# A graph layer and a routed feed-forward layer on one core: message rows gathered before they are normalized, full expert tiles started from eight queues, results scattered out between the gathers

## The chip, the cores and the metric

The kernel runs on one core of one Trainium2 chip. The metric is the device time in microseconds (us) of one execution; the time of a kernel is the median of its runs.

## The reference

All values are 32-bit floats. There are 12,500 nodes with 256 features and 212,500 edges, sorted by destination.

```python
x = x + gnn(layernorm(x))
x = x + ffn(layernorm(x))

def gnn(features):                      # src, dst, edge_weight: 212500 each
    msgs = features[src] * edge_weight[:, None]
    agg = segment_sum(msgs, dst, 12500)
    return agg @ W.T + b

def ffn(h):                             # 8 experts, 256 -> 1024 -> 256
    idx = argmax(softmax(h @ gate_w + gate_b));  prb = that probability
    pos = place of the token among those of its expert, in order
    y = relu(h @ w1[idx] + b1[idx]) @ w2[idx] + b2[idx]
    return nan_to_num(y * prb * (pos < capacity))
```

## The kernel before

Nodes are handled in 98 tiles of 128. The edges are cut into 98 groups of 17 columns of 128 edges, and each group into three thirds of 6, 6 and 5 columns. The kernel has these parts:

- **Normalizing x (prologue).** SP loads batches of 7 tiles of x, DVE takes their moments (`moments`, L1076 and L1081), ACT scales them (`normalize`, L786) and stores them to the DRAM tensor `normed`. POOL clears the accumulator `aggT` (L688) meanwhile. POOL waits until all of `normed` is stored and for the flag of a check of the edge lists (L690, L691) before its first gather.
- **Aggregation.** For each column, POOL issues one indirect DMA (`gather`, L707) that fetches 128 rows of `normed` into `msg`. DVE copies the indices into `idx` (L1193) and builds the weighted one-hot matrices of a third with two operations (`prep`, L1195, L1199). PE multiplies (`sub`, L939), ACT copies the sums out (`pair_out`, L846), PE transposes them (L948) and DVE adds them to `aggT` (L1216).
- **Node.** For a finished tile PE multiplies by W (`gnn`, L957), DVE adds x and bias and normalizes (L1225 to L1241), PE transposes (L966) and computes the gate (L972), DVE chooses the expert (`route_a`) and works out the row (`route_b`, L1264 to L1276), and POOL scatters the tile's rows into the DRAM tensor `rows_by_expert` (`scatter`, L714). SP stores the sum x + gnn to the DRAM tensor `x_after_gnn` (L621).
- **Experts.** The 98 node tiles form four segments of 25, 25, 25 and 23. When a segment is routed, DVE plans it (`planning`), and its expert tiles (118 slots with padding in all) run beside the gathers of the next segment: rows loaded by SP into `hin` (L573), transposed on PE (L990), layer 1 (L999), relu on ACT (L810), layer 2 (L1011), bias on DVE (L1290), and stored by ACT to one of the DRAM tensors `expert_outputs` (L826). Weights are loaded by SP (L584) into one of two slots of `wsl` if the expert changes. `hin` has two buffers too; a row load waits for the transpose two tiles before (`s_ft`, L572).
- **Combining.** After the last segment is planned, six node tiles at a time: SP loads `x_after_gnn` (L629), POOL gathers the rows of `expert_outputs` (L735), DVE multiplies and adds (L1302), ACT checks for NaN (L834) and stores to the output (L837).

The order of work is written out in Python by `steps_of`, and every engine walks the same list (`walk`). Each engine executes its own instructions strictly in that order, and a wait on a semaphore holds up everything behind it on its engine. `s_route` tells POOL that a tile's rows have their places; `s_y` that an expert tile's result is in `yrow`.

Of the kernel before, what the change touches and what calls it, by code (L numbers as in the profile page):

```python
# [5 lines left out]
P = 128  # L13
# [6 lines left out]
WIN = 64  # L20
LAG = 2
# [3 lines left out]
EXTRA = 2  # L25
LN_TILES = 7
LN_BUFS = 4
MOST_FINS = 6

C_IDENT, C_TRI, C_IOTA, C_HALVES, C_ODD, C_RANK, C_SEG = 0, 128, 256, 320, 384, 448, 456  # L30


def segments_of(tiles):

    if tiles >= 90:
        last = [25, 25, 23]
        return [tiles - sum(last)] + last
    return [tiles - tiles // 2, tiles // 2]
# [6 lines left out]
def layout_of(n, e, experts):  # L45

    tiles = -(-n // P)
    edge_tiles = -(-e // P)
    group = -(-edge_tiles // tiles)
    third = -(-group // 3)  # L50
    subs = [third, third, group - 2 * third]
    halves = [[-(-n // 2), n // 2] for n in subs]
    seg = segments_of(tiles)
    caps = [P * (t + 1) for t in seg]
    base = [0]
    for c in caps:
        base.append(base[-1] + (experts + 1) * c)
    columns = -(-(n + WIN) // WIN) * WIN

    fins = min(MOST_FINS, columns // (4 * P))  # L60
    return dict(tiles=tiles, aggregate=columns, fins=fins, group=group, subs=subs, halves=halves, seg=seg, caps=caps, base=base,
                columns=(tiles + 1) * group, ffn=[t + experts - 1 for t in seg])


def buffer_of(s, last):

    return 2 if s == last else min(s, 1)


def paces_of(products, iterations):  # L70

    for pattern in ([2, 3, 3], [3, 3, 3], [4, 4, 3], [4, 4, 4]):
        paces = [2] + [pattern[j % 3] for j in range(iterations - 1)]
        if sum(paces) >= products:
            return paces
    return paces


def steps_of(tiles, seg, ffn, per_step):

    steps = [dict(agg=0), dict(agg=1)]  # L90
    node = f = k0 = place = 0
    last = len(seg) - 1
    ends = [seg[0], sum(seg[:last]), tiles]
    products, paces = [], [0] * tiles

    def plan_products(s):

        end = k0 + ffn[s] - EXTRA
        for k in range(k0, end):
            first = [("turn", k)] if k == k0 else []  # L100
            ahead = k + 2 < end
# [20 lines left out]
    for s, t in enumerate(seg):  # L122
        for j in range(t):
# [3 lines left out]
            if node:  # L127
                it["rank"] = node - 1
# [1419 lines left out]
```

## Time and profile before

| | us |
|---|---|
| median of 3 runs | 2694.51 (2691.34 to 2696.41) |
| the profiled execution, its own time | 2699.82 |
| its span, first to last instruction | 2697.8 |
| first gather starts | 127.98 |
| last gather starts | 2361.51 |
| POOL busy | 1822.4 (68% of the span) |
| PE busy | 1910.5 (71%) |
| mean granted TensorE clock | 0.822 |

A row of a table of groups reads: line, engine, operation, what is written <- what is read, shape, how often | busy us, mean ns of one | idle time of the engine just before them and what ended it. A row of a timeline reads: start, duration, engine, line, operation, how often, and in brackets the idle time before and its releaser. PEld is the load of weights into PE, SPq and ACTq are the issue of a DMA by SP and ACT. Busy shares are averages over stages with different limits, so the rows below are taken stage by stage.

### The profile page before, as it was taken

How to read it: one execution, taken by the hardware profiler on the slowest of the kernel's cores; microseconds unless marked ns; L12 is line 12 of the kernel's file. 1: busy time of each engine (PE TensorE's matmuls, PEld its weight loads, DVE VectorE, ACT ScalarE, POOL GpSimd, SP SyncE). 2: the span in 40 equal slices, each digit the busy share in tenths (PEclk: the TensorE clock that was granted, in tenths of full speed). 3: DMA queues.
4: the chain of work that ended last, by engine and by line, in shares of the span. 5: the costliest groups of instructions: out<-in, count | busy, mean ns of one | idle time of the engine just before them, and what ended most of it. 6: DMA issues, size and time to landing. Idle time of an engine off the chain costs nothing. (4 is left out here: it accounts for less than half of the span.)

```text
span 2697.8 us, 41267 instructions
## 1 busy us (share of the span) xinstructions
PE 1910.5 (71%) x11208; PEld 1430.3 (53%) x11208; DVE 1157.6 (43%) x4700; ACT 853.0 (32%) x2232; POOL 1822.4 (68%) x1867
## 2 busy tenths in 40 slices
PE   0045556666568888888678888887688888849992
PEld 0023333333346666666466666665467666638882
DVE  6524443443454444444444444444544444442222
ACT  2502221222223333333233333333233333314443
POOL 3077777777777777777777777777777777722333
PEclk9976665555569898988689889898798999969996
DMA  5733333333366464455465644654665446447775
GB/s 202 263 109 115 116 116 115 117 116 116 116 203 198 132 198 130 132 194 163 132 231 167 197 130 132 196 165 124 213 195 198 138 143 207 142 110 248 241 270 155
DMA packets 207538, 444.34 MB, mean 165 GB/s; under 512 B 48332, under 2 KB 133572, under 8 KB 197372
## 3 DMA queue, kind: packets, MB, share of 16 engines
q0 software_dynamic: 89376, 244.09, 30.7%
q1 hardware_dynamic: 84744, 156.38, 16.9%
q10 hardware_dynamic: 33172, 41.08, 4.2%
q8 instruction: 95, 1.56, 0.2%
q14 instruction: 151, 1.24, 0.1%
HBM read 374.71 MB, written 72.43 MB: 166 GB/s over the span
## 5 line engine op out<-in xcount | busy, mean ns | idle before, releaser
L707 POOL DMA_INDIRECT msg<-normed,idx x1666 | 1604.1, 963 | 613.4 <-issue 507.3
L939 PE MATMUL ps_agg<-msg,onehot 128*64 128x256 f32 x3332 | 611.2, 499 | 501.1 <-DMA msg<-normed,idx 458.6
L939 PEld LDWEIGHTS ps_agg<-msg,onehot 128*64 128x64 f32 x3332 | 288.0, 171 | 718.9 <-DMA msg<-normed,idx 540.4
L999 PE MATMUL ps_h<-hTf,wsl 128*128 128x128 f32 x3776 | 473.4, 286 | 3.9 <-DVE hTf L1283 3.9
L999 PEld LDWEIGHTS ps_h<-hTf,wsl 128*128 128x128 f32 x3776 | 459.4, 202 | 25.4 <-issue 18.7
L1011 PE MATMUL ps_y<-wsl,hmid 128*128 128x256 f32 x1888 | 444.6, 390 | 5.3 <-ACT hmid L810 5.3
L1011 PEld LDWEIGHTS ps_y<-wsl,hmid 128*128 128x128 f32 x1888 | 362.0, 197 | 54.9 <-issue 7.3
L1216 DVE TENSOR_TENSOR aggT<-aggT,ps_agg 128x128 f32 x588 | 169.6, 288 | 488.8 <-PE ps_agg L948 253.5
L810 ACT ACTIVATE hmid<-ps_h,wsl 128x128 f32<-128x128 f32 x944 | 268.3, 370 | 311.7 <-PE ps_h L999 305.9
L846 ACT COPY pairs<-ps_agg 128x256 f32<-128x256 f32 x294 | 107.9, 367 | 655.6 <-PE ps_agg L939 655.3
L1193 DVE COPY idx<-src_sb 128x6 int32<-128x6 int32 (+1 forms) x297 | 68.4, 230 | 422.4 <-PE ps_agg L939 415.7
L735 POOL DMA_INDIRECT aggT<-expert_outputs,yidx x98 | 98.6, 1006 | 178.6 <-DVE yidx L1295 110.5
L1290 DVE TENSOR_TENSOR yrow<-ps_y,wsl 128x256 f32<-128x256 f32 x118 | 50.0, 424 | 303.1 <-issue 149.5
L867 ACT ACT_TABLE_LOAD x97 | 124.5, 1283 | 136.7 <-DVE yrow L1290 135.4
L1199 DVE TENSOR_TENSOR onehot<-onehot,wgt 128x384 f32<-128x384 f32 (+1 forms) x297 | 160.0, 539 | 10.2
L948 PE MATMUL ps_agg<-cst,pairs 128*128 128x128 f32 x588 | 137.4, 321 | 30.2 <-ACT pairs L846 30.0
L1195 DVE TENSOR_TENSOR onehot<-cst,rel 128x384 f32<-128x384 f32 (+1 forms) x297 | 157.1, 529 | 0.0
L714 POOL DMA_INDIRECT rows_by_expert<-hrow,slot_i x98 | 98.3, 1003 | 67.5 <-DVE slot_i L1276 38.6
L857 ACT COPY aggS<-aggT 128x256 f32<-128x256 f32 x98 | 39.6, 404 | 280.1 <-DVE aggT L1216 280.1
L957 PE MATMUL ps_x<-wg_sb,aggS 128*128 128x256 f32 x392 | 126.6, 455 | 0.0
L860 ACT ACT_TABLE_LOAD x98 | 125.7, 1283 | 2.6 <-ACTq L887 0.9
L948 PEld LDWEIGHTS ps_agg<-cst,pairs 128*128 128x128 f32 x588 | 84.4, 169 | 76.1 <-ACT pairs L846 67.0
(130 smaller groups left out, 1501.8 us busy)
## 6 DMA issues: line engine op xcount, KB each, us to landing
wsl<-in_w SPq DMA_DIRECT2D x72, 1024.0 KB
msg<-normed,idx POOLq DMA_INDIRECT x1666
hin<-rows_by_expert SPq DMA_DIRECT2D x118, 128.0 KB
expert_outputs<-yrow ACTq DMA_DIRECT2D x118, 128.0 KB, 2.5
xt<-in_x SPq DMA_DIRECT2D x97, 128.0 KB
x_after_gnn<-xt SPq DMA_DIRECT2D x97, 128.0 KB
aggT<-x_after_gnn SPq DMA_DIRECT2D x97, 128.0 KB, 3.8
out_x<-aggT ACTq DMA_DIRECT2D x97, 128.0 KB, 2.9
```

Source lines behind the costliest of these rows:

```text
L707: pool.indirect_dma_start(out=msg[:, j, :], out_offset=None, in_=ln_dram, in_offset=bass.IndirectOffsetOnAxis(ap=idx[:, j:j + 1], axis=0)) ...
L810: ins = nc.scalar.activation(hmid[:, c, :], ps_h[:, c, :], ACT.Relu, bias=b1_at(b)[:, c:c + 1])
L860: nc.scalar.activation(rt[:, 2 * E8:3 * E8], rt[:, E8:2 * E8], ACT.Exp, accum_out=sc[:, 1:2]).then_inc(s_exp, 1)
L867: nc.scalar.activation(sd[:, :], mv[:, 1:2], ACT.Sqrt, bias=eps[:, 0:1]).then_inc(s_sd, 1)
L939: ins = nc.tensor.matmul(ps_agg[h * WIN:(h + 1) * WIN, q % 2, 0:D], onehot[:, j, :], msg[:, j, :], start=i == 0, stop=i == HALVES[q][h] - 1)
L948: last = nc.tensor.transpose(ps_agg[:, q % 2, D + k * P:D + (k + 1) * P], pairs[:, q % 2, k * P:(k + 1) * P], ident)
L957: last = nc.tensor.matmul(ps_x2[:, 0:D], aggS[:, k, :], wg_sb[:, k, :], start=k == 0, stop=k == KD - 1)
L999: last = nc.tensor.matmul(ps_h[:, c, :], w1_at(b)[:, q, c * P:(c + 1) * P], hTf[:, q, :], start=q == 0, stop=q == KD - 1)
L1011: last = nc.tensor.matmul(ps_y[:, 0:D], hmid[:, c, :], w2_at(b)[:, c, :], start=c == 0, stop=c == FC - 1)
L1195: dve.tensor_tensor(hot, iota.unsqueeze(1).to_broadcast([P, n, WIN]), rel[:, bass.ds(col, n)].unsqueeze(2).to_broadcast([P, n, WIN]), ALU. ...
L1199: dve.tensor_tensor(hot, hot, wgt[:, bass.ds(col, n)].unsqueeze(2).to_broadcast([P, n, WIN]), ALU.mult).then_inc(s_onehot[q], 1)
L1216: dve.tensor_tensor(columns, columns, half, ALU.add).then_inc(s_added[q] if h else s_half, 1)
```

## The change

The kernel's file is rewritten in large part; what it computes is the same.

- **Start.** POOL's first gathers wait only for the first 34 columns of the indices. The first 12 groups (36 thirds, 204 gathers) fetch rows of `x` itself; DVE takes the moments of each gathered row and ACT normalizes it in `msg` (`message_moments`, `normalize_messages`). Meanwhile x is normalized to `normed` in 25 batches of 4 tiles, interleaved with these thirds; from third 36 on the gathers fetch from `normed`. ACT and DVE clear `aggT`.
- **Aggregation.** `msg` is a ring of four thirds. Gathers take their index straight from `src_sb`. The one-hot matrix of a column is 32 wide and made by one `tensor_scalar` with two scalars per row (17 for a group), four quarters of a third are multiplied side by side, and the transpose becomes a product with a shift matrix (`turn`), so that one addition per third goes to `aggT`.
- **Nodes.** They start at third 38, one every two thirds until they have caught up (node 32, about third 104), then one every three thirds. Rows are 260 wide: x + gnn, its two normalizing factors, the gain and the node's number; POOL scatters them into eight queues in DRAM, one per expert. `x_after_gnn` goes.
- **Experts.** There are no segments. A visit v takes 128 rows of one queue: `plan` (11 small DVE operations) picks the fullest queue, or the one of two visits before while it still has 128 rows, whose weights are then kept. Visits start with node 13; each takes two thirds (layer 1, layer 2): one every two thirds up to third 104, then one for a node, and from node 68 on five for four nodes. There are 105 visits; in the list of events 85 of them (0 to 84) have their layer 2 inside the 294 thirds, and 20 (85 to 104) after the last third. Before visit 89, SP writes 8 pads of 384 rows behind the queues.
- **Result.** DVE forms the output rows (`combine`, two operations) and POOL scatters them straight into the output by the node's number, with a bounds check that drops padding; 84 of these scatters stand between the gathers, two thirds after the visit. `expert_outputs`, its gathers and the combining stage go.

After the last third the list of events repeats, for each visit v: `z v`, second weights v+2, rows v+2 (`hl`), normalize the rows v+2 (`hn`), `l1 v+1`, first weights v+3, plan, transpose v+2 (`tf`), `l2 v+1`, `z v+1`. `l1` stands for layer 1 on PE and its relu on ACT, `z` for `combine`. The core of the diff:

```diff
-WIN = 64
-LAG = 2
-EXTRA = 2
+QWIN = 32
+TWIN = 96
+RAW_GROUPS = 12
+LN_TILES = 4
+LAG_TILES = 14
+HOLD = 5
+ROW = 260
+RING = 4
+POOL_LAG = 2
...
+    def rest():
+        if not pending and queue:
+            v, _ = queue.pop(0)
+            pending.extend([("l1", v), ("l2", v)])
+        if pending:
+            kind, v = pending.pop(0)
+            if kind == "l1":
+                for do in ("hl", "hn", "tf"):
+                    once(do, v)
+                if queue:
+                    once("hl", queue[0][0])
+                    once("hn", queue[0][0])
+            elif queue:
+                for do in ("hl", "hn", "tf"):
+                    once(do, queue[0][0])
+            events.append((kind, v))
+            if kind == "l2":
+                events.append(("z", v))
...
+            def rows(v):
+                sp.wait_ge(s_plan, v + 1)
+                row = sp.snap(sp.value_load(plan_i[0:1, 4 * v + 1:4 * v + 2], min_val=0, max_val=ROWS - P))
+                if v < FULL:
+                    scattered_to(sp, AFTER[v])
+                else:
+                    scattered_to(sp, NT - 1)
+                    sp.wait_ge(s_pads, 16 * E8)
+                    sp.wait_ge(s_gate, 80)
+                if v >= 2:
+                    sp.wait_ge(s_z, v - 1)
+                sp.dma_start(hin[:, v % 2, :], hbuf[bass.ds(row, P), :]).then_inc(s_hin[v % 2], 16)
+            def weights(v, signal, to, source):
+                expert = sp.snap(sp.value_load(plan_i[0:1, 4 * v:4 * v + 1], min_val=0, max_val=E8 - 1))
+                keep = sp.value_load(plan_i[0:1, 4 * v + 2:4 * v + 3], min_val=0, max_val=1)
+                with sp.If(keep < 1):
+                    sp.dma_start(to, source[bass.ds(expert, 1)].rearrange("e p c -> p (e c)")).then_inc(signal, 16)
+                with sp.Else():
+                    sp.sem_inc(signal, 16)
+            def weights1(v):
+                sp.wait_ge(s_plan, v + 1)
+                if v >= 2:
+                    sp.wait_ge(s_relu, 2 * (v - 1))
+                weights(v, s_w1[v % 2], wsl[:, v % 2, 0:W1], wfirst)
+            def weights2(v):
+                sp.wait_ge(s_plan, v + 1)
+                if v >= 2:
+                    sp.wait_ge(s_z, v - 1)
+                weights(v, s_w2[v % 2], wsl[:, v % 2, W1:W1 + W2], wsecond)
...
+            def pad_queues():
+                sp.wait_ge(s_padrow, 1)
+                for e in range(E8):
+                    row = sp.snap(sp.value_load(pad_i[0:1, e:e + 1], min_val=0, max_val=ROWS - PADS))
+                    scattered_to(sp, NT - 3)
+                    sp.dma_start(hbuf[bass.ds(row, PADS), :], pads).then_inc(s_pads, 16)
...
+            def gather(t):
+                g, q, u, m = third(t)
+                if t >= RING:
+                    pool.wait_ge(s_mm[u], summed(t - RING))
+                for j in range(SUBS[q]):
+                    col = g * G + OFF[q] + j
+                    pool.indirect_dma_start(
+                        out=msg[:, m + j, :], out_offset=None, in_=x if t < RAW else ln_dram,
+                        in_offset=bass.IndirectOffsetOnAxis(ap=src_sb[:, col:col + 1], axis=0)).then_inc(s_msg[u], 16)
...
+            def output(v):
+                pool.wait_ge(s_z, v + 1)
+                pool.indirect_dma_start(
+                    out=out, out_offset=bass.IndirectOffsetOnAxis(ap=ids[:, v:v + 1], axis=0),
+                    in_=result(v), in_offset=None, bounds_check=N - 1, oob_is_err=False).then_inc(s_out, 16)
...
+            for t in range(T):
+                if t == RAW:
+                    general()
+                gather(t)
+                for n in routed.get(t, ()):
+                    if n < NT - 3:
+                        scatter(n)
+                for v in combined.get(t, ()):
+                    output(v)
+                    stored = v + 1
+            for n, first in ((NT - 3, 0), (NT - 2, 0), (NT - 1, V)):
+                scatter(n)
+                while stored < V and first:
+                    output(stored)
+                    stored, first = stored + 1, first - 1
...
+            def expert_norm(v):
+                act.wait_ge(s_hin[v % 2], weights_used(v))
+                if v:
+                    act.wait_ge(s_ft, v)
+                row = hin[:, v % 2, :]
+                nc.scalar.activation(hf[:, :], row[:, 0:D], ACT.Identity, bias=row[:, X_NMR:X_NMR + 1],
+                                     scale=row[:, X_RSTD:X_RSTD + 1]).then_inc(s_hf, 1)
...
+            def aggregate(t):
+                g, q, u, m = third(t)
+                if t < RAW:
+                    pe.wait_ge(s_norm, t + 1)
+                else:
+                    pe.wait_ge(s_msg[u], arrived(t))
+                if t >= 2:
+                    pe.wait_ge(s_added, t - 1)
+                for i in range(QUARTERS[q][0]):
+                    for h in range(4):
+                        if i < QUARTERS[q][h]:
+                            j = m + QOFF[q][h] - OFF[q] + i
+                            last = nc.tensor.matmul(ps[h * QWIN:(h + 1) * QWIN, t % 2, 0:D], onehot[:, j, :],
+                                                    msg[:, j, :], start=i == 0, stop=i == QUARTERS[q][h] - 1)
+                            if i == QUARTERS[q][h] - 1:
+                                last.then_inc(s_mm[u], 1)
...
+            def message_moments(t):
+                g, q, u, m = third(t)
+                dve.wait_ge(s_msg[u], arrived(t))
+                if t >= 2:
+                    dve.wait_ge(s_norm, t - 1)
+                small = raw_small[:, t % 2, 0:SUBS[q], :]
+                for j in range(SUBS[q]):
+                    link.mark(dve.bn_stats(small[:, j, 0:6], msg[:, m + j, :]))
+                link.wait()
+                for j in range(SUBS[q]):
+                    last = dve.bn_aggr(small[:, j, 6:8], small[:, j, 0:6])
+                last.then_inc(s_rawmv, 1)
...
+                g, q, u, m = third(t)
+                n, col = SUBS[q], g * G + OFF[q]
+                if t >= RING:
+                    dve.wait_ge(s_mm[u], summed(t - RING))
+                if t == 0:
+                    dve.wait_ge(s_wgt, 16)
+                for j in range(n):
+                    last = dve.tensor_scalar(onehot[:, m + j, :], iota[:, 0:QWIN], rel[:, col + j:col + j + 1],
+                                             wgt[:, col + j:col + j + 1], ALU.is_equal, ALU.mult)
+                last.then_inc(s_onehot, 1)
...
+            def add(t):
+                first = dve.snap(dve.value_load(base_i[0:1, t:t + 1], min_val=0, max_val=N - 1))
+                dve.wait_ge(s_turned, t + 1)
+                if t == 0:
+                    dve.wait_ge(s_zero, 1)
+                    link.wait()
+                else:
+                    dve.wait_ge(s_added, t)
+                columns = aggT[:, bass.ds(first, TWIN), :].rearrange("p c k -> p k c")
+                dve.tensor_tensor(columns, columns, ps[:, t % 2, D:D + KD * TWIN].rearrange("p (k c) -> p k c", k=KD),
+                                  ALU.add).then_inc(s_added, 1)
...
+            def combine(v):
+                row = hin[:, v % 2, :]
+                dve.wait_ge(s_hin[v % 2], weights_used(v))
+                link.mark(dve.tensor_copy(ids[:, v:v + 1], row[:, X_ID:X_ID + 1]))
+                dve.wait_ge(s_w2[v % 2], weights_used(v))
+                dve.wait_ge(s_l2, v + 1)
+                link(dve.tensor_tensor(tbuf[:, :], ps[:, Y, 0:D], b2_at(v % 2), ALU.add))
+                dve.wait_ge(s_n1, min(v + 1, NT))
+                link(dve.scalar_tensor_tensor(out=result(v), in0=tbuf[:, :], scalar=row[:, X_GAIN:X_GAIN + 1],
+                                              in1=row[:, 0:D], op0=ALU.mult, op1=ALU.add, accum_out=fin[:, v:v + 1]))
+                dve.sem_inc(s_z, 1)
```

## Rows read from the trace of the kernel before

**Rows 1.** Busy by stage: from:to, us, busy of PE, PEld, DVE, ACT, POOL, clock, DMA share, GB/s.
```profile
200.00:700.00 500.00, 294.22 (x1188) 158.19 (x1188) 201.87 (x860) 112.09 (x223) 379.66 (x396) 0.59 0.39 116
800.00:2360.00 1560.00, 1276.94 (x8088) 998.49 (x8088) 714.50 (x2941) 538.49 (x1390) 1186.48 (x1226) 0.89 0.53 168
...
2410.00:2620.00 210.00, 184.33 (x1232) 170.60 (x1233) 55.98 (x204) 85.46 (x327) 72.95 (x72) 0.95 0.77 258
```
**Rows 2.** Groups of instructions on POOL.
```profile
L707 POOL DMA_INDIRECT msg<-normed,idx x1666 | 1604.1, 963 | 613.4 <-issue 507.3 <-DVE idx L1193 106.1
L735 POOL DMA_INDIRECT aggT<-expert_outputs,yidx x98 | 98.6, 1006 | 178.6 <-DVE yidx L1295 110.5 <-ACTq L887 33.7 <-issue 24.1
L714 POOL DMA_INDIRECT rows_by_expert<-hrow,slot_i x98 | 98.3, 1003 | 67.5 <-DVE slot_i L1276 38.6 <-issue 28.9
```
**Rows 3.** Timeline of POOL: first gathers, one long one, last gather, last scatter.
```profile
127.98 1.12 POOL L707 DMA_INDIRECT msg<-normed,idx  x1 [106.12 <-DVE idx L1193]
...
132.08 0.95 POOL L707 DMA_INDIRECT msg<-normed,idx  x1 [0.30 <-issue]
...
400.78 1.23 POOL L707 DMA_INDIRECT msg<-normed,idx  x1 [0.30 <-issue]
...
2361.51 1.02 POOL L707 DMA_INDIRECT msg<-normed,idx  x1 [0.30 <-issue]
...
2404.34 0.93 POOL L714 DMA_INDIRECT rows_by_expert<-hrow,slot_i  x1 [9.07 <-DVE slot_i L1276]
```
**Rows 4.** Timeline of the start: POOL's clearing, the cast, one batch normalized.
```profile
0.75 21.11 POOL L688 MEMSET aggT<- 128x25216 f32 x1 [0.29 <-POOLq L1541]
...
5.32 17.43 DVE L1099 CAST rel<-msg 128x1683 f32<-128x1683 int32 x1 [3.87 <-DMA msg<-in_dst_t]
...
35.39 2.38 DVE L1076 BATCH_NORM_STATS2 fix<-wsl 128x6 f32<-128x256 f32 x7 [0.44 <-DVE fix L1089]
37.92 0.57 DVE L1081 BATCH_NORM_AGGREGATE fix<-fix 128x2 f32<-128x6 f32 x7
...
38.83 3.53 ACT L786 ACTIVATE wsl<-wsl,fix 128x256 f32<-128x256 f32 x7
```
**Rows 5.** Timeline of DVE: the index copy alone, beside a gather, and the one-hot product.
```profile
127.36 0.17 DVE L1193 COPY idx<-src_sb 128x6 int32<-128x6 int32 x1
...
400.11 0.36 DVE L1193 COPY idx<-src_sb 128x5 int32<-128x5 int32 x1 [1.46 <-PE ps_agg L939]
...
400.71 0.49 DVE L1199 TENSOR_TENSOR onehot<-onehot,wgt 128x320 f32<-128x320 f32 x1
```
**Rows 6.** Groups of instructions on ACT and DVE.
```profile
L867 ACT ACT_TABLE_LOAD x97 | 124.5, 1283 | 136.7 <-DVE yrow L1290 135.4
...
L1257 DVE TENSOR_SCALAR rt<-cst,sc 128x8 f32<-128x8 f32 x98 | 25.1, 256 | 3.9 <-DVE sc L1256 0.5
```
**Rows 7.** Timeline of expert tiles of the last segment on ACT, PE, SP and DVE.
```profile
2502.73 1.14 ACT L810 ACTIVATE hmid<-ps_h,wsl 128x128 f32<-128x128 f32 x4 [0.58 <-PE ps_h L999]
2502.75 3.62 PE L1011 MATMUL ps_y<-wsl,hmid 128*128 128x256 f32 x16
...
2506.20 0.35 SPq L584 DMA_DIRECT2D wsl<-in_w  x1
2506.46 0.42 DVE L1290 TENSOR_TENSOR yrow<-ps_y,wsl 128x256 f32<-128x256 f32 x1 [3.09 <-PE ps_y L1011]
...
2508.69 0.34 SPq L584 DMA_DIRECT2D wsl<-in_w  x1
...
2510.50 0.34 SPq L573 DMA_DIRECT2D hin<-rows_by_expert  x1
...
2519.56 0.44 PE L990 MATMUL ps_in<-cst,hin 128*128 128x128 f32 x2 [1.61 <-DMA hin<-rows_by_expert]
```
**Rows 8.** Timeline: the last gather of results and the operation that uses it.
```profile
2681.27 1.16 POOL L735 DMA_INDIRECT aggT<-expert_outputs,yidx  x1 [0.30 <-issue]
...
2684.42 0.48 DVE L1302 SCALAR_TENSOR_TENSOR aggT<-aggT,gain 84x256 f32<-84x256 f32 x1 [0.91 <-DMA aggT<-expert_outputs,yidx]
```

More of the change, by code:

```diff
@@ L170, with visits_after @@
-MOVING = ("agg", "node", "rank", "fin", "done")
-def gnn_moe_kernel(nc, x, src_t, dst_t, w_t, w_gnn, b_gnn, gate_w, gate_b, w1, b1, w2, b2, consts, limits,
-                   zeros, out, sizes):
+    quarters = [[(m + 3 - h) // 4 for h in range(4)] for m in subs]
+    columns = -(-(n + TWIN) // GWIN) * GWIN
+    queue = -(-(n + PADS) // P) * P
+    return dict(tiles=tiles, group=group, subs=subs, quarters=quarters, columns=columns, queue=queue)
+def visits_after(tiles, experts, n):
+    lag = LAG_TILES
+    late = tiles - 3
+    slack = experts - 1
+    turn = late - 4 * (lag - slack)
+    if n <= turn:
+        return max(0, n + 1 - lag)
+    return min(n + 1 - slack, turn + 1 - lag + -(-5 * (n - turn) // 4))
@@ L803, in _, with normalize_messages @@
[L803 to L806 removed]
+                act.wait_ge(s_lny, b + 1)
+                for t in range(ln_parts(b)):
+                    act.dma_start(ln_dram_rows(ln_dram, b, t), ln_sbuf_rows(b, t)).then_inc(s_lnst[u], 16)
+            def normalize_messages(t):
+                g, q, u, m = third(t)
+                act.wait_ge(s_rawsc, t + 1)
+                for j in range(SUBS[q]):
+                    row = msg[:, m + j, :]
+                    last = nc.scalar.activation(row, row, ACT.Identity, bias=raw_small[:, t % 2, j, 9:10],
+                                                scale=raw_small[:, t % 2, j, 8:9])
+                last.then_inc(s_norm, 1)
@@ L829, in check @@
-            def check(tiles):
-                for f, place, used in tiles:
-                    r = rows_of(f)
-                    hold(act, "act", s_fin, f + 1)
-                    nc.scalar.activation(junk[0:r, :], xg_at(place)[0:r, :], ACT.Copy, scale=0.0,
-                                         accum_out=finite_col(f, r)).then_inc(s_checked, 1)
-                    hold(act, "act", s_checked, f + 1)
-                    act.dma_start(out[bass.ds(f * P, r), :], xg_at(place)[0:r, :]).then_inc(s_out[place], 16)
@@ L983, in ranks, with turn_rows @@
+                nc.tensor.matmul(ps[:, TR, D + 2 * E8:D + 3 * E8], ones[0:r, :], choice, start=True, stop=True
                                  ).then_inc(s_rank, 1)
-            def turn_ffn(k, b):
-                hold(pe, "pe", s_hin[b], half(k, b) * 16 + 16)
-                if not (known(k) and k == 0):
-                    hold(pe, "pe", s_hTf, k)
-                for q in range(KD):
-                    last = nc.tensor.transpose(ps_in[:, q * P:(q + 1) * P], hin[:, b, q * P:(q + 1) * P], ident)
+            def turn_rows(v):
+                pe.wait_ge(s_hf, v + 1)
+                if v:
+                    pe.wait_ge(s_hTf, v)
+                for k in range(KD):
+                    last = nc.tensor.transpose(ps[:, IN, k * P:(k + 1) * P], hf[:, k * P:(k + 1) * P], ident)
```

1920 lines of the change are left out of this document (846 added, 1074 removed).

## The prediction

> **What bounds the kernel now.** I read the table of groups by line first, then busy time by stage, then the timelines of POOL, of the start and of the end. POOL issues 1,666 gathers of 963 ns on average, and nearly all of its idle time before them is 0.30 us of "issue" each [rows 2]; single ones stand 1.25 us apart [rows 3]. From the first gather (127.98) to the last (2361.51) POOL issues 1,666 gathers and 94 scatters, so 1,759 steps of 1.270 us. It waits for nobody there, while DVE is busy 0.40 to 0.46 and PE 0.59 to 0.82 of the time [rows 1]. So there are three pieces: a start of 128 us in which x is normalized, 2,234 us set by the number of POOL's instructions, and an end of 336 us: the last three nodes (43 us from last gather to last scatter [rows 3]), then expert tiles with PE busy 0.88 of the stage [rows 1], then the last results.
>
> **Start of the gathers.** The first gather waits only for a small load. The load of `dst_t`, the first in SP's queue now and 800 KB, is there when DVE uses it at 5.32 [rows 4]; a smaller one should be there at 3.5. That takes 124.5 us from the first piece.
>
> **POOL's queue.** Up to the last gather it now holds 1,666 gathers, 95 scatters of nodes and 84 scatters of results: 1,845 instructions, 85 more than before, and no waits on loaded indices. What one with a bounds check costs the trace doesn't show; the nearest rows are the scatter (1.003 us) and the gather of results (1.006 us) [rows 2]. From below the cost is a plain gather's 0.95, from above I take 2.0 us (+84 us in all), and I choose the like of L714, since a comparison of an index is small beside writing 128 descriptors. The mean step of 1.270 has 0.019 of long instructions in it: some hundred take 1.2 us [rows 3], and the one at 400.78 starts inside a one-hot product of DVE [rows 5]. Those products go, the new `tensor_scalar`s come; I keep 1.270, with 1.25 as the lower end (-37 us). So the last gather starts at 3.5 + 1,844 x 1.270 = 2345.4, if nothing holds POOL up.
>
> **What can hold POOL up.** A gather waits until PE has multiplied the third four places back. Three places:
>
> At the start POOL has filled the ring after 23 gathers, at about 33 us. DVE must first clear, cast, subtract and build three one-hots, then take moments; the 17.43 us of the cast last just until POOL's clearing of 21 us ends [rows 4], and that clearing goes to ACT and DVE. I add up 33 us to the first scaling and 5.5 us for ACT and PE: a stall of 6 us.
>
> In the 36 raw thirds DVE takes per row 2.38 / 7 = 0.34 for the statistics and 0.57 / 7 = 0.08 for the aggregate [rows 4], so 2.4 us for 5.67 rows; 0.83 of a batch of four tiles at 0.42 each plus 0.5, 1.8 us; two scales 0.5; 5.67 one-hots at 0.23 (0.256 in [rows 6], overlapped a little), 1.3 us; shift, addition and semaphores 1.1. That is 7.1 us against POOL's 5.67 x 1.270 = 7.2. ACT's 0.50 a row [rows 4] makes 5.7. It just fits; the check of the lists at third 6 (some 7 us) doesn't: 5 us lost. The branch at third 36: 2 us.
>
> From third 76 to 104 there are a node and a visit in two thirds, for which POOL needs 13.33 x 1.270 = 16.9 us. Here the engines' order makes a circle: DVE's route(n-1) lets PE turn node n (0.4), then layer 2 (3.7), gate and turn (0.9), then DVE's addition (0.4), combine (1.1), plan (2.2), one-hots (1.4), choice (1.3), node with its wait for ACT, which loads a table of 1.28 us twice [rows 6] (3.3), shift and addition (0.7), one-hots (1.4), route (1.1): 17.9 us. 14 pairs lose 1.0 each: 14 us. Between 0 and 40 is open. Elsewhere a node has three thirds, 24 us, against 15 on DVE and 18 on PE. Results are scattered two thirds (14 us) after a visit that is done some 10 us into them, so they should be there.
>
> Last gather: 2345.4 + 6 + 5 + 2 + 14 = 2372.4, later than before.
>
> **The end.** Three nodes alone took 43 us [rows 3]; now visits 85 and 86 lie between their steps. I take 42 us to the end of visit 86: 2414.4. Then 18 visits remain, where before 28 tiles were done after the last gather and then the combining of 98.
>
> Their pace is not PE's. In the list of events "rows v+2" and "normalize rows v+2" stand before "layer 1 of v+1". The rows v+2 go into the buffer that z(v) reads, so SP loads them after z(v); and ACT, which is in order, can't do the relu of v+1 before it has normalized them. So every result waits for a load that is issued after the result before. Counted from z(v): SP sees the signal and issues second weights after 1.6 (from the end of L1290 at 2506.88 to 2508.69 it is 1.8), and rows 1.3 to 1.8 later (2510.50) [rows 7], at 3.0. They were there at 2519.56, 9.1 us after issue, behind two weight loads of 1 MB. Here the same two lie before them, the first issued 2 us before z(v): 2.1 MB at 258 GB/s [rows 1] are 8 us. I take the landing at 7.6. Then 0.45 to normalize, 1.25 for four relus, 3.7 for layer 2, 1.3 for two DVE operations and signals [rows 7, 8]: 14.3 us. Where weights are kept, 12.2. Few experts still have 256 rows then, so I take 12 visits of the 17 at 14.3 and 5 at 12.2: 232.6. The last has no rows to wait for: 8.4. Sum 2655.4.
>
> The Trainium skill (DMA: Bandwidth & Descriptors, Queues, rings and completion order) says that each DMA engine consumes the descriptors of one issuing queue in ring order, which would put the rows wholly behind the weights. The 9.1 us agree with that.
>
> After the last z a scatter and its landing take 4.3 us (1.16 in issue, next use 3.15 after its start [rows 8]) where before there was a check and a store; the span ended 12.9 us after its last result (2684.90 to 2697.8). I take 14: 2669.4, and the 2.0 us around the span: 2671.4. The profiled execution took 2699.8, 5.3 above the median, so the change is -28.4, and on the median's scale 2666.
>
> **Rivals.**
>
> A. *The end is paced by PE.* If rows arrive in time after all (SP faster, weights mostly kept), a visit takes what a tile takes now: 1,232 records of PE in 210 us at 50 a tile (32 of layer 1, 16 of layer 2, 2 of the transpose) is 8.5 us [rows 1]. For: PE is free otherwise. Against: the order just read. 17 x 8.5 = 144.5 in place of 232.6: 2578.
>
> B. *DVE paces the thirds (slower than before).* A copy of 5 or 6 columns takes 0.17 alone and up to 0.36 beside a gather, and the cast waited for the memset [rows 4, 5]: POOL and such DVE operations exclude each other. The change makes 1,666 short ones of them. If each takes 0.43 in place of 0.23, a raw third takes 8.2: 36 x 1.1 - 4 = 36 us, and a pair of the crowded stage 2.3 more: 32 us. 2734. From 0.07 us more for each it decides: then the gain is gone. Against: only the window in the middle of an instruction of POOL blocks, most copies take 0.17 to 0.25.
>
> The Trainium skill (SBUF — State Buffer, Who interferes with whom) says that a DVE operation in a two-port mode, `tensor_scalar` among them, and a GpSimd operation hold the shared port pair exclusively for the whole instruction. By that the 1,666 operations of 0.23 us could cost POOL up to 383 us; all long instructions of POOL together cost 30 us here, and DVE's 294 index copies were in its way just as short, so the trace bears out the exclusion but only a small part of such a price.
>
> C. *Results are not there when POOL comes to them.* Then the 84 scatters stall gathers behind them; at 1 us each 84 us, 2750. Against: 4 us to spare by the count above. It counts with B.
>
> **Numbers.** Forecast 0.50, itself 2630 to 2705 (POOL's step, stalls, landing at 6 to 9 us); A 0.15; B and C 0.25; a shorter queue at 1.25 a step without A, 2630, 0.10. The change can be told from none by 0.2%, 2689 to 2700. Faster: 0.15 + 0.08 + 0.37 of the forecast's 0.50 = 0.60; within it 0.10; slower 0.25 + 0.03 + 0.02 = 0.30. The range leaves out the ends of A and of B: 2560 to 2745.
>
> **What would show it.** First gather before 5 us; steps of 1.27 us; 7 us between thirds up to third 36; the last gather at 2345 to 2400. After it, PE idle some 40% with ACT's relus waiting for a DMA into `hin`, and 14 us from one combine to the next. The prediction is wrong if combines follow at 8.5 us, if POOL waits for PE or DVE over long stretches, or if result scatters take much over 1.0 us.

## The result and the profile after

| | before | after |
|---|---|---|
| median | 2694.51 us (2691.34 to 2702.38, 5 runs) | 2711.07 us (2710.32 to 2712.68, 5 runs) |
| span of the profiled execution | 2697.8 | 2709.3 |
| first gather | 127.98 | 2.89 |
| last gather | 2361.51 | 2379.83 |
| last gather to the end of the span | 336.3 | 329.5 |

The ratio is 1.0057, 95% interval 1.0041 to 1.0073: the change makes the kernel slower by some 0.6%. The forecast was 2666 and faster. The time lies inside the whole range of 2560 to 2745 and 6 us above the forecast's own 2630 to 2705; the sign is wrong.

The spans add up as -125.1 (start) + 143.4 (from first to last gather) - 6.8 (end) = +11.5 us. The middle piece grew by the 84 instructions more on POOL, some 1.25 us each (105 us), and by 48.5 us in which POOL waits; what its instructions take beyond 0.947 us each came to 21.5 us in place of 31.9, 10 us less.

POOL's groups after the change (line, operation, times | busy us, mean ns | idle before and its releaser) answer to [rows 2]:

```profile
L568 POOL DMA_INDIRECT msg<-normed,src_sb x1462 | 1393.9, 953 | 448.4 <-issue 443.0 <-DVEq L1221 4.0 <-PE ps L811 1.4
L568 POOL DMA_INDIRECT msg<-in_x,src_sb x204 | 197.5, 968 | 88.3 <-issue 54.5 <-PE ps L811 31.3 <-DMA src_sb<-in_src_t 2.4
L600 POOL DMA_INDIRECT out_x<-aggT,ids x98 | 97.4, 994 | 206.9 <-DVEq L1221 175.1 <-issue 31.8
L594 POOL DMA_INDIRECT rows_by_expert<-xrow,slot_i x98 | 96.4, 984 | 71.8 <-issue 28.6 <-DVEq L1181 26.7 <-DMA rows_by_expert<-in_pads 16.1
```

The scatter of results, L600, has a bounds check and takes 0.99 us, so the chosen like of L714 was right. Most of its 175 us of waiting lies after the last gather.

POOL's timeline (start, duration, ..., idle before and its releaser) answers to [rows 3]: the start, the first waits, the four results around 850 us, the last gather.

```profile
2.89 1.12 POOL L568 DMA_INDIRECT msg<-in_x,src_sb  x1 [2.45 <-DMA src_sb<-in_src_t]
...
6.83 3.08 POOL L568 DMA_INDIRECT msg<-in_x,src_sb  x1 [0.30 <-issue]
...
38.47 0.94 POOL L568 DMA_INDIRECT msg<-in_x,src_sb  x1 [2.91 <-PE ps L811]
...
93.84 0.95 POOL L568 DMA_INDIRECT msg<-in_x,src_sb  x1 [11.05 <-PE ps L811]
...
219.35 0.94 POOL L568 DMA_INDIRECT msg<-in_x,src_sb  x1 [1.34 <-PE ps L811]
227.26 0.94 POOL L568 DMA_INDIRECT msg<-in_x,src_sb  x1 [0.70 <-PE ps L811]
...
822.49 0.99 POOL L600 DMA_INDIRECT out_x<-aggT,ids  x1 [1.49 <-DVEq L1221]
840.82 1.00 POOL L600 DMA_INDIRECT out_x<-aggT,ids  x1 [2.23 <-DVEq L1221]
860.02 0.99 POOL L600 DMA_INDIRECT out_x<-aggT,ids  x1 [3.01 <-DVEq L1221]
878.15 1.00 POOL L600 DMA_INDIRECT out_x<-aggT,ids  x1 [0.78 <-DVEq L1221]
...
2379.83 0.95 POOL L568 DMA_INDIRECT msg<-normed,src_sb  x1 [0.30 <-issue]
```

The reader sees a POOL that almost always steps by 0.95 + 0.30 us, waits 11.05 us once at the check of the lists, 1.4 us beyond the usual 0.30 in every three raw thirds, and up to a few us before results in the crowded stage, where the results shown follow each other by 18.1 to 19.2 us and not by POOL's 16.9.

The end of the changed kernel: one visit, from combine (L1217) to combine. It answers to [rows 7].

```profile
2534.08 0.42 DVE L1217 TENSOR_TENSOR tbuf<-ps,wsl 128x256 f32<-128x256 f32 x1 [11.64 <-PE ps L903]
...
2536.54 0.34 SPq L505 DMA_DIRECT2D wsl<-in_wsecond  x1
...
2537.96 0.34 SPq L499 DMA_DIRECT2D hin<-rows_by_expert  x1
2542.49 0.60 ACT L720 ACTIVATE hf<-hin 128x256 f32<-128x256 f32 x1 [12.44 <-DMA hin<-rows_by_expert]
2543.00 2.16 ACT L734 ACTIVATE hmid<-ps,wsl 128x128 f32<-128x128 f32 x8
2543.14 0.69 PE L883 MATMUL ps<-cst,hf 128*128 128x128 f32 x2 [5.60 <-ACT hf L720]
2544.26 5.91 PE L903 MATMUL ps<-wsl,hmid 128*128 128x256 f32 x16 [0.43 <-ACT hmid L734]
...
2550.29 0.42 DVE L1217 TENSOR_TENSOR tbuf<-ps,wsl 128x256 f32<-128x256 f32 x1 [12.85 <-PE ps L903]
```

ACT's relu of this visit stands behind the normalization of the next rows, the rows land 7.5 us after the result before is finished (2535.03, the end of L1219), and PE has nothing to do for 5.6 us. All this was forecast. What was not is the 5.91 us of layer 2. Busy times of the engines in parts of this visit, with the granted clock as the third number from the end:

```profile
2533.60:2537.60 4.00, 3.94 (x34) 3.72 (x32) 2.76 (x18) 0.00 (x0) 0.97 (x1) 1.00 0.49 195
2537.60:2543.10 5.50, 0.00 (x0) 0.00 (x0) 0.00 (x0) 0.61 (x2) 0.00 (x0) 0.90 0.73 253
2544.30:2547.30 3.00, 3.00 (x7) 2.45 (x8) 0.00 (x0) 1.11 (x5) 0.00 (x0) 0.50 0.00 0
2547.30:2550.20 2.90, 2.90 (x12) 2.39 (x11) 0.00 (x0) 0.00 (x0) 0.00 (x0) 0.75 0.88 298
```

PE was idle from 2537.6 to 2543.1; when layer 2 starts, the granted clock is 0.50, the 1.2 GHz level of the 2.4 GHz clock, and it comes back only in the second half. DMA moves nothing in the first half (0.00), so no load beside layer 2 is what slows it. The table of waits from 2425 to 2700 (engine, line waited in <- for: us in total, times, longest) and the busy times of that stretch:

```profile
ACT hf L720 <- DMA hin<-rows_by_expert: 218.9, 17, 13.8
DVE tbuf L1217 <- PE ps L903: 218.6, 18, 14.8
...
PE ps L883 <- ACT hf L720: 90.1, 17, 6.0
```

```profile
2425.00:2700.00 275.00, 177.56 (x893) 150.19 (x893) 47.05 (x303) 52.03 (x178) 20.44 (x21) 0.78 0.41 142
```

In this stretch the granted clock is 0.78 and DMA is busy 0.41, against 0.95 and 0.77 in the end of the kernel before [rows 1]. Combines stand at 2424.63 and 2693.59 with 17 steps between them: 15.82 us a visit, and ACT waits for rows once in each of the 17.

### The profile page after: what moved, and what is told of

Its sections match the earlier page's. It is cut to its first block, busy times and chain, and to the rows that moved or that the text cites. A ratio compares the mean times of both kernels' runs of the same rounds, so it can differ in the third digit from the quotient of the medians.

```text
span 2709.3 us, 41004 instructions
## 1 busy us (share of the span) xinstructions
PE 1862.1 (69%) x11158; PEld 1393.2 (51%) x11158; DVE 1329.3 (49%) x6884; ACT 1011.7 (37%) x2393; POOL 1792.3 (66%) x1873
## 4 chain that ended last, share of the span: by engine, by line
POOL 44%; issue 19%; PE 14%; DVE 12%; DMA 5%; ACT 5%; SPq 1%; DVEq 0%; POOLq 0%; ACTq 0%
POOL msg L568 39%; PE ps L903 9%; ACT msg L685 3%; DMA hin<-rows_by_expert 3%; POOL rows_by_expert L594 3%; DVE wsl L1055 2%; POOL out_x L600 2%; DMA msg<-normed,src_sb 2%; PE ps L820 2%; DVE onehot L1071 2%; PE ps L811 1%; ACT hmid L734 1%; DVE aggT L1219 1%; DVE tbuf L1217 1%; DVE wsl L1058 1%
## 5 line engine op out<-in xcount | busy, mean ns | idle before, releaser
L568 POOL DMA_INDIRECT msg<-normed,src_sb x1462 | 1393.9, 953 | 448.4 <-issue 443.0
L811 PE MATMUL ps<-msg,onehot 128*32 128x256 f32 x3332 | 436.6, 513 | 453.5 <-DMA msg<-normed,src_sb 428.0
L891 PEld LDWEIGHTS ps<-hTf,wsl 128*128 128x128 f32 x3360 | 463.5, 224 | 54.5 <-issue 53.6
L903 PE MATMUL ps<-wsl,hmid 128*128 128x256 f32 x1680 | 477.0, 447 | 7.6 <-ACT hmid L734 7.6
L891 PE MATMUL ps<-hTf,wsl 128*128 128x128 f32 x3360 | 479.2, 310 | 0.0
L903 PEld LDWEIGHTS ps<-wsl,hmid 128*128 128x128 f32 x1680 | 375.8, 230 | 110.9 <-issue 47.2
L1071 DVE TENSOR_SCALAR onehot<-cst,rel,wgt 128x32 f32<-128x32 f32 x1666 | 378.7, 325 | 14.5 <-DVE plan_i L1208 4.2
L820 PE MATMUL ps<-shift,pairs 128*128 128x96 f32 x1176 | 232.0, 329 | 155.7 <-ACT pairs L694 155.7
L734 ACT ACTIVATE hmid<-ps,wsl 128x128 f32<-128x128 f32 x840 | 235.4, 371 | 132.3 <-PE ps L891 132.3
L568 POOL DMA_INDIRECT msg<-in_x,src_sb x204 | 197.5, 968 | 88.3 <-issue 54.5
L600 POOL DMA_INDIRECT out_x<-aggT,ids x98 | 97.4, 994 | 206.9 <-DVEq L1221 175.1
L1217 DVE TENSOR_TENSOR tbuf<-ps,wsl 128x256 f32<-128x256 f32 x105 | 43.7, 417 | 229.0 <-PE ps L903 228.9
L594 POOL DMA_INDIRECT rows_by_expert<-xrow,slot_i x98 | 96.4, 984 | 71.8 <-issue 28.6
```

What stands on the lines that cost most here:

```text
L568: pool.indirect_dma_start(out=msg[:, m + j, :], out_offset=None, in_=x if t < RAW else ln_dram, in_offset=bass.IndirectOffsetOnAxis(ap=src ...
L594: pool.indirect_dma_start(out=hbuf, out_offset=bass.IndirectOffsetOnAxis(ap=slot_i[0:r, n % 2:n % 2 + 1], axis=0), in_=xrow[0:r, n % 3, :] ...
L600: pool.indirect_dma_start(out=out, out_offset=bass.IndirectOffsetOnAxis(ap=ids[:, v:v + 1], axis=0), in_=result(v), in_offset=None, bounds ...
L734: last = nc.scalar.activation(hmid[:, c, :], hps(c), ACT.Relu, bias=b1_at(v % 2)[:, c:c + 1])
L811: last = nc.tensor.matmul(ps[h * QWIN:(h + 1) * QWIN, t % 2, 0:D], onehot[:, j, :], msg[:, j, :], start=i == 0, stop=i == QUARTERS[q][h] - 1)
L820: last = nc.tensor.matmul(ps[:, t % 2, D + k * TWIN:D + (k + 1) * TWIN], pairs[:, t % 2, k * P:(k + 1) * P], shift[:, t % 2, :], start=Tru ...
```

## The experiments

Each ratio is to the kernel before, run beside the variant on the same chip. "The step" is the mean of the visits of the end, combine to combine, as above. Line numbers of a variant differ by a few from those of the changed kernel.

**1. The order of the end.** The rows of the next visit are normalized after this visit's layer 2 and result; they are still loaded into the same two buffers.

```diff
                 if queue:
                     once("hl", queue[0][0])
-                    once("hn", queue[0][0])
-            elif queue:
-                for do in ("hl", "hn", "tf"):
-                    once(do, queue[0][0])
             events.append((kind, v))
```

> Only the order of the last visits changes: normalize and transpose of the next visit's rows stand after layer 2 and combine of this one, no longer before its relu. Theory (every result of the end waits for a load of rows issued after the result before): a visit takes layer 1 3.7 + layer 2 3.6 + transpose, copy and signals 1.6 = 8.9 us in place of 16.2 between combines, 17 of them save 115 to 125 us: about 2590 us. Rival 1 (the end is paced by 2.2 MB of weights a visit at the 142 GB/s that the stage shows): no change, 2700 to 2711. Rival 2 (most of the loss is TensorE's low clock there): layer 2 stays at 5 to 6 us and a visit at 11 us or more, about 2630 or above.

Measured: 2594.8 us (2590.09 to 2599.06), ratio 0.9618 (0.9595 to 0.9641). The last gather is where it was (2378.57), the step falls from 15.82 to 9.08. Waits and busy times between 2425 and 2575:

```profile
ACT hmid L730 <- PE ps L887: 50.0, 33, 3.8
ACT hf L716 <- DMA hin<-rows_by_expert: 32.7, 14, 3.8
```

```profile
2425.00:2575.00 150.00, 130.94 (x818) 115.82 (x816) 42.83 (x275) 53.53 (x166) 17.49 (x18) 0.97 0.74 258
```

ACT waits mostly for PE now, PE is busy 0.87 of the time at a granted clock of 0.97. The place of two steps (normalize and transpose) in a list of events cost the changed kernel 116 us. Layer 2 takes 3.62 us in all 17 visits; no long idle time of PE stands before it any more. (Layer 1 takes 5.5 us in three of them in place of 3.84, see 5.)

**2. A third buffer, the order as it was.** From visit 88 on, rows go round three buffers (the third is a free place of `msg`) and are loaded one visit earlier.

```diff
                     once(do, queue[0][0])
+                if len(queue) > 1:
+                    once("hl", queue[1][0])
...
-                    sp.wait_ge(s_z, v - 1)
+                    sp.wait_ge(s_z, v - 1 if v < 88 else v - 2)
```

> The order of the last visits is kept, but their rows have a third buffer (in the message ring, free by then) from visit 88 on, and are loaded before combine v, not after it. Theory: the rows are there when ACT wants them, a visit takes PE's 3.7 + 3.6 + 0.4 and signals, 8.2 to 9.2 us, about 2585 to 2600 us. Rival 1 (weights pace the end): no change. Rival 2 (the order of ACT's and PE's work alone makes the wait, whatever the load): no change either, while e1 changes.

Measured: 2607.67 us (2604.75 to 2610.52), ratio 0.9668 (0.9649 to 0.9686); last gather 2378.56, step 9.55. So the loss needs both halves: the order that puts the next rows ahead of this relu, and the buffer that frees only with the result. Taking away either gives back most of it. ACT still waits for rows here (66.2 + 34.2 us in 150, against 32.7 with the reordering), and in four of the 17 visits layer 2 still takes 5.1 to 5.4 us; both fit the 13 us by which the reordering gains more.

**3. PE kept busy.** 20 products whose results nobody reads follow layer 1 of each visit from 88 on; the wait for rows stays.

```diff
                     layer1(key[0])
+                    if 88 <= key[0] < V - 1:
+                        pe.wait_ge(s_added, T)
+                        for _ in range(20):
+                            nc.tensor.matmul(ps[:, 0, 0:P], ident, tri, start=True, stop=True)
```

> 20 idle products of two constant matrices (4.3 us of PE at the full clock) stand after layer 1 of the visits 88 to 103, where PE now waits 5.6 us for the rows; their result is not used. Theory with the clock as its second part: layer 2 falls from 5.1 to 6.0 us to 3.6 to 3.7, the rows arrive as before, so 16 visits save 1.5 to 2.3 each: 2675 to 2687 us. Rival (layer 2 is slow for another reason, such as its weights landing beside it): layer 2 stays at 5 to 6 us and the time at 2709 to 2715.

Measured: 2693.47 us (2688.24 to 2703.53), ratio 0.9989 (0.9977 to 1.0001), step 14.57, 11 of the 17 at 13.5 to 14.3. More work makes the kernel some 17 us faster. PE's timeline in it:

```profile
2513.63 4.63 PE L931 MATMUL ps<-cst 128*128 128x128 f32 x40
2519.15 0.44 PE L883 MATMUL ps<-cst,hf 128*128 128x128 f32 x2 [0.89 <-ACT hf L720]
2520.27 3.69 PE L903 MATMUL ps<-wsl,hmid 128*128 128x256 f32 x16 [0.68 <-ACT hmid L734]
```

Layer 2 takes 3.69 us in this visit and the transposition 0.44 in place of 0.69, at a granted clock of 0.95 between 2425 and 2575. Of the 16 visits with idle products, 12 have layer 2 at 3.6 to 3.7 us and four at 5.3 to 5.4; in three of these four PE still idled 2.1 to 2.6 us at once, in the 12 at most 1.4. The rows are there no earlier than before, mostly 7.0 to 7.8 us after the result and twice 8.4 and 8.5. The idle time of PE thus costs twice: by itself, and by the slow layer 2 behind it.

**4. Results last.** All 105 scatters of results are issued after the last node's scatter (in the changed kernel 84 of them stand between gathers); the end's order is as in the change.

```diff
                 elif kind == "z":
-                    combined.setdefault(now + POOL_LAG, []).append(key[0])
+                    combined.setdefault(T + now, []).append(key[0])
```

> None of the 84 result scatters stands between the gathers; POOL issues all 105 behind the last node's scatter, where it is idle 9 tenths of the time. Theory (the middle is paced by the number of POOL's instructions): 84 x 1.27 = 107 us and the 22 us that POOL waited for results are gone, PE's and DVE's circle of 18.5 us for two thirds in the crowded stage gives back 15 to 40 of it: last gather at 2265 to 2290 in place of 2380, 2595 to 2620 us. Rival (the circle or PE paces much of the middle, and the scatters are hidden): last gather above 2340, 2670 us or more.

Measured: 2625.83 us (2623.91 to 2627.36), ratio 0.973 (0.9711 to 0.9748); the last gather starts at 2282.25, 97.6 us earlier, and the step is 16.2. POOL has idle time enough in the end to issue the 84 there. Its waits in the crowded stage don't vanish: where 21.6 us stood before results, 36.8 us now stand before the scatters of rows.

**5. Both edits, 1 and 4.**

> The changed kernel with both edits at once: rows of the next visit normalized after layer 2 and z of this one, and all 84 results scattered after the last node. If the two gains are separate (the end's pace of 9.1 us a visit in place of 15.8, 17 visits: 114 us; the last gather at 2282 in place of 2380, with the end starting that much earlier but holding some twelve result scatters more): 2282 + some 45 to the first visit of the end + 17 x 9.1 + one scatter after the other of results 1.3 us each, most of them under the visits, + 10 = some 2500 to 2520, ratio 0.93. If what the gathers gain is lost again because PE's work is now the bound (the end starts when PE comes, not when POOL comes): above 2560.

Measured: 2522.33 us (2520.89 to 2524.91), ratio 0.9355 (0.9335 to 0.9376). The last gather starts at 2278.23; the step is 10.46 and not 9.1. The gains nearly add: 2522.3 where separate ones would give 2509.6. Between 2331 and 2509 ACT waits 50.0 us for rows, up to 6.5 at once, at 272 GB/s; the results that now go out beside the loads are a likely cause, not tested. The slow clock is not gone for good either. Where PE idled 2.4 to 4.9 us at a time, the work behind it is now layer 1, and in six of the 17 visits it takes 5.3 to 6.4 us in place of 3.84, 11 us in all:

```profile
2388.69 0.69 PE L879 MATMUL ps<-cst,hf 128*128 128x128 f32 x2 [4.02 <-ACT hf L716]
2389.84 5.63 PE L887 MATMUL ps<-hTf,wsl 128*128 128x128 f32 x32 [0.46 <-ACT hTf L723]
...
2399.60 3.84 PE L887 MATMUL ps<-hTf,wsl 128*128 128x128 f32 x32 [0.46 <-ACT hTf L723]
```

**6. The crowded stage.** There a node and a visit came every two thirds. Three edits take different parts of what could hold POOL there. (a) The nodes are 2 and 3 thirds apart in turn:

```diff
-        t = max(t + 2, 3 * (n + 2))
+        t = max(t + 2 + n % 2, 3 * (n + 2))
```

> The changed kernel with the nodes of the crowded stage 2 and 3 thirds apart in turn in place of 2 and 2, nothing else (the end's order and the time of the result scatters as in the change). Theory (a circle of 18 to 18.5 us for which two thirds of POOL leave 16.9): POOL's 21.7 us of waits before outputs fall under 6, the last gather comes at some 2358 to 2364, the end keeps 15.8 us a visit, time some 2692, ratio 0.998 to before. If the stage's length is set by something other than node and visit in one circle, the waits stay at 15 or more and the time at 2705 to 2711.

Measured: 2692.06 us (2688.84 to 2695.28), ratio 0.9987 (0.9976 to 0.9997). POOL's waits before results between 670 and 880 are gone (21.6 us to 0), the last gather starts at 2358.3, the step stays at 15.6.

(b) The one-hots of a third by two long operations, as before the change, in place of five or six `tensor_scalar`s:

> The changed kernel with each third's one-hots built by two tensor_tensor operations, as the kernel before does it, in place of five or six tensor_scalars. Theory (the crowded stage is a circle of DVE, PE and ACT and its length is the stall): six tensor_scalars took 1.33 us, two long operations some 1.1 to 1.4, so the stall of 22 us between 670 and 880 changes by less than 15 us and the time by less than 0.5%. Rival B of the prediction (the short tensor_scalars and POOL lock each other out of a port): POOL's time above 0.947 us an instruction, 22.6 us now, falls to under 10, and the gathers of the unstalled stretches step by 1.25 in place of 1.29; 30 us or more faster. If the port is held rather by the long tensor_tensors, that excess goes up to 30 as it was before and the kernel is slower by 8 us.

Measured: 2693.99 us (2687.45 to 2696.86), ratio 0.9994 (0.9982 to 1.0005); last gather 2362.68, waits of the crowded stage 4.3 us. The waits fell by 17.4 us, more than the expected under 15. In DVE's timeline of this kernel a third's one-hots take 0.75 us:

```profile
845.24 0.36 DVE L1071 TENSOR_TENSOR onehot<-cst,rel 128x192 f32<-128x192 f32 x1
845.63 0.36 DVE L1073 TENSOR_TENSOR onehot<-onehot,wgt 128x192 f32<-128x192 f32 x1
```

In the changed kernel six `tensor_scalar`s take 1.33 us, or 1.47 where they lie badly to an instruction of POOL:

```profile
848.00 1.47 DVE L1071 TENSOR_SCALAR onehot<-cst,rel,wgt 128x32 f32<-128x32 f32 x6
...
2220.78 1.33 DVE L1071 TENSOR_SCALAR onehot<-cst,rel,wgt 128x32 f32<-128x32 f32 x6
```

And POOL's gathers don't notice which form stands beside them, 953 ns as after the change:

```profile
L568 POOL DMA_INDIRECT msg<-normed,src_sb x1462 | 1393.7, 953 | 448.2 <-issue 441.4 <-DVEq L1222 5.5 <-PE ps L811 1.3
```

So it is the length of the circle that DVE shortens, and not a port that POOL had to wait for. On DVE's side the exclusion is there, but small: in the changed kernel the 287 `tensor_scalar`s that start 0.40 to 0.62 us after an indirect DMA of POOL has started take 0.45 us on average, the others 0.30, and they still start 0.21 us apart (median). All groups of five and six together lose 9 us by it.

Only where DVE's one-hots lie in the circle does the shorter form help. In the raw thirds it gives nothing: POOL's waits between 45 and 240 us are 18.5 us with the short operations and 19.7 with the two long ones. From 110 to 290 DVE is busy 120.1 us in place of 135.0, and what it saves it spends waiting for the turned sums. One addition, after the change and in this variant:

```profile
255.46 0.36 DVE L1093 TENSOR_TENSOR aggT<-aggT,ps 128x192 f32 x1 [1.99 <-PE ps L820]
```

```profile
255.22 0.36 DVE L1094 TENSOR_TENSOR aggT<-aggT,ps 128x192 f32 x1 [2.67 <-PE ps L820]
```

(c) Each result scattered three thirds after its visit in place of two (`POOL_LAG + 1`). It ran twice. On the chip of the first run the kernel before itself took 3521.47 us and the variant 3601.51, ratio 1.0235 (1.019 to 1.028), with POOL waiting for routes in every stage. What slowed that chip is not known, and nothing is concluded from this run.

> The changed kernel with each result scattered three thirds after its visit in place of two; nothing else. If POOL's 21.7 us before outputs between 670 and 880 are results that come just too late (rival C in small), but the gathers behind them then run into the same circle of DVE, PE and ACT: the waits before outputs vanish, some 10 us of them come back before the rows' scatter or the gathers, the last gather comes 5 to 20 us earlier than 2379.8, the time is 2690 to 2706. If the later scatter costs nothing and the circle leaves room: 22 us faster, 2689. If the circle alone sets the pace: no change, 2711, with the same 22 us before other instructions. The end keeps its 15.8 us a visit in each case.

> The kernel with each result scattered three thirds after its visit, again, since the kernel before itself took 3521 us on the chip of the first run. The same three cases: some 10 of the 21.7 us of waits before outputs come back before other instructions, time 2690 to 2706 beside some 2695 of before; or all are gained, 2689; or none, 2711. The end keeps 15.8 us a visit.

Measured the second time: 2704.87 us (2701.77 to 2709.97), ratio 1.0034 (1.0024 to 1.0045). POOL's waits of the stage are 17.1 us in place of 21.6: 6.0 before results, 11.1 now before rows (L594 waiting for the route). The lateness of the results is a symptom, the circle the cause.

**7. All that helped.** The edits of 1, 4 and 6a together, and then with 6b too.

> The kernel with both edits (order, results last) and the nodes of the crowded stage one after the other by 2 and 3 thirds in turn in place of 2 and 2. If the stall there (36.8 us with results last) comes from a circle of node and visit that is longer than two thirds of POOL, it falls under 10 us and the last gather comes 20 to 35 us earlier than in the kernel with both edits alone, 2250 to 2262, the time with it, ratio 0.92. If POOL is held there by the single result of PE (route waiting for turn within each node, however far apart the nodes are), the stall keeps its 3 us a node and the time stays within 8 us of the kernel with both edits.

> The kernel with both edits and the spread nodes, and the one-hots by two tensor_tensor operations. As between the changed kernel and the one with two-operation one-hots: within 10 us of the spread kernel if the form of the one-hots matters little; more than 20 us faster if tensor_scalars hold POOL's port.

Measured: 2485.01 us (2483.49 to 2486.41), ratio 0.922 (0.92 to 0.9241), and with the two-operation one-hots 2490.1 us (2485.07 to 2495.73), ratio 0.9242 (0.9215 to 0.9269). The last gathers start at 2244.53 and 2248.02, and neither has a wait left in the crowded stage; the 33.6 us that experiment 5 lost there are gained whole. Without waits to remove, the two-operation form is no faster: its last gather comes 3.5 us later, and POOL's instructions up to it take 17.6 us beyond 0.947 us each in place of 13.0. The two times are too close to be told apart by four runs each. The better of the two beats the kernel before by 7.8% and the changed kernel by 8.3%. Its end, busy times from 2296 to 2446:

```profile
2296.00:2446.00 150.00, 120.17 (x735) 106.80 (x736) 40.97 (x245) 47.60 (x146) 95.70 (x99) 0.93 0.84 300
```

## Why the prediction was wrong in its sign

**Which step failed.** The size of a visit in the end: "3.7 for layer 2 ... 14.3 us. Where weights are kept, 12.2 ... 12 visits of the 17 at 14.3 and 5 at 12.2: 232.6". Measured: 269.0, that is 36 us more, and more than the 28 us that the forecast was ahead of the kernel before. The mechanism was the one named, rows that wait for the result before; two numbers in it were off. The 3.7 us of layer 2 came from [rows 7], where PE hardly paused (busy 0.88 at a granted clock of 0.95 [rows 1]); here it follows an idle time of 5.6 us and took 4.99 to 6.53, 5.8 on average: 36 us over 17 visits. And 16 of the 17 visits loaded second weights, not 12, 2.1 us each: 8 us. The landing was mostly 7.1 to 7.5 in place of 7.6, and the signals were shorter: -8 us, as what is left of the sum. All other terms of the forecast's span were off by 3.5 us together, so the error in the end was enough to turn the sign. Experiment 3 shows the first point: with PE kept busy, layer 2 falls to 3.69 us in most visits, its excess over 17 visits from 36 to 8 us, and the span from 2709.3 to 2686.4.

The Trainium skill (TensorE: Matmul & The Clock Gate, Part 1, What's actually happening) says that the clock's default is the throttled level and activity releases it, back to full when busy and down when idle. The rows of the visit above agree: 1.00, idle, then 0.50. The prediction had all it needed for it, an idle time in each visit and a stage at a granted clock of 0.59 [rows 1], and priced the work behind it as if the clock stayed.

**Point by point.**

| step | predicted | measured |
|---|---|---|
| first gather | 3.5 | 2.89 |
| last gather if nothing holds POOL | 2345.4 | 2331.3 (2379.83 - 48.5), a step of 1.263 |
| waits of POOL beyond 0.30: start | 6 | 2.6 |
| check at third 6 | 5 | 10.8 |
| other raw thirds | 0 | 10.6 |
| branch at third 36 | 2 | 2.7 |
| crowded stage | 14 | 21.6 |
| last gather | 2372.4 | 2379.83 |
| result of visit 86 finished | 2414.4 | 2425.6 |
| 17 visits | 232.6 | 269.0 |
| last visit | 8.4 | 7.0 |
| from there to the end | 14 | 7.7 |
| span | 2669.4 | 2709.3 |

The check of the lists takes 8.2 us on DVE (84.14 to 92.3) and comes before the one-hots for which PE waits, so it is lost nearly whole on top of a wait that was already there. In the raw thirds the count of DVE's work, 7.1 us against POOL's 7.2, was called "just fits". A third took 7.6 us, but not because DVE was full: between 110 and 290 it waits 0.6 to 3.5 us in each third for the turned sums. What fills a third is a circle that the prediction didn't add up, here and also with shorter one-hots (experiment 6b): moments and aggregates on DVE (2.5 us), a square root (0.3) and scaling on ACT (2.6 to 3.1), the copy of the sums (0.35), the turning on PE (1.2), the addition (0.4), then the next moments. The two errors before the last gather (POOL's step -14, waits +21) cancel in part. The forecast also took 5 us off for the median's scale, which the changed kernel didn't repeat: its median is 2711.07 at a span of 2709.3.

**The rivals.** A, an end paced by PE, didn't happen in the changed kernel, but its price was right: experiment 1 makes it so and measures 9.08 a visit against 8.5. B, the port: the 1,666 `tensor_scalar`s stand 0.22 us apart and not 0.43, and neither gathers nor the step are slowed. They do meet POOL, for some 9 us of DVE's time in the whole kernel, but POOL's gathers don't grow (953 ns), where the prediction had 383 us as the most that it could cost POOL. But its second half held: it named the crowded stage as the place where slower one-hots decide, and experiment 6b moves 17 us there. C, results not there: in the crowded stage only, 22 us of waits and not 84. Experiments 6a and 6c show that it is the circle of node and visit that is late and not the place of the scatter: spreading the nodes gives back all 21.6, a later scatter 4.7.

**Where the expected gain went.** 125 us were won at the start. 84 scatters between gathers gave back 105 of them (experiment 4: the last gather 98 earlier, the kernel 85 us faster), for work that POOL could do beside the end. The end, with 21 results of expert tiles after the last gather in place of 30 and no combining stage, should have been much shorter; it was 6.8 us shorter, because each visit waits for its rows (experiment 1: 116 us).

## What to carry to other kernels

Where one engine's instruction count sets the pace, put on it only what must go there, and leave the rest for a stage in which it idles: 84 scatters moved behind the gathers gave 85 us of the kernel's time. In a list of events that every engine walks in order, look for a step of item v+2 ahead of a step of item v+1 that waits on it, and for the buffer that it needs; either alone costs little (steps of 9.1 and 9.55 us), both together made a visit 15.8 us. When a forecast says that PE idles in each round, here by 5.6 us, price the work behind the idle time at the lower clock. And when an engine seems just to fit, look for the circle through the other engines: in the raw thirds DVE had idle time, and each third was still too long.

## What the hardware showed unexpectedly

Idle products on PE made the kernel faster (ratio 0.9989 against 1.0057), though they sit in 16 of the last visits. A `tensor_scalar` of DVE is lengthened by POOL mainly if it starts 0.4 to 0.6 us into an indirect DMA (0.45 us against 0.30), and the gathers are 953 ns long whichever form stands beside them. Two of the first gathers took 3.08 us (at 6.83) and 2.69 us (at 17.73) in place of 0.95; DVE cleared and cast beside the first and ran a row of `tensor_tensor`s beside the second. What lengthened them wasn't tried. The bounds check of an indirect scatter costs nothing that shows: 0.99 us with it (L600), 0.98 without (L594).
